# Third attention's scores computed once, masked keys overwritten instead of masked by a matmul, weights in two transfers, and a new order of the stages

## The reference

```python
# layer 0: 16 heads of 16 channels; keys are the 64 context tokens and the 64 latents (x)
h = concat([ctx, x]); q = x @ q_w + q_b; k, v = split(h @ kv_w + kv_b)
attn = where(concat([mask, ones]), q k / 16, -inf)      # masked context keys drop out
x = norm(softmax(attn) v @ out_w + ...) -> gelu MLP -> + x
# layer 1: token-mixing block: layer norm, five mixes, r, k, v, w, g, a scan over the tokens,
#          group norm, output product, a second norm and a gated feed-forward
# layer 2: softmax(q k / 16) over the context, one head, folded weights
# layer 3: 32 query heads of 8 channels, 8 key heads
scores = q k / sqrt(8) + attention_mask; attn = softmax(scores); out = attn v @ Wo + bo
x = layernorm(out + x) * gamma + beta
```

## Time and profile before

| | |
|---|---|
| runs | 1628.13, 1628.97, 1629.14 us, median 1628.97 |
| the profiled execution | 1628.69 us, of which 1626.5 us from the first to the last instruction |
| busy in the span | PE 1459.5 us (90%), DVE 958.1 (59%), ACT 626.7 (39%), POOL 649.4 (40%) |
| granted TensorE clock, mean | 0.964 |
| chain that ended last | PE 71%, DVE 10%, ACT 7%, POOL 7% |

### The profile page before, as it was taken

One profiled execution on the slowest core, in us unless ns is written; L12 is line 12 of the kernel. 1 busy time (PEld: TensorE's weight loads), 2 busy tenths in 40 slices (PEclk: granted clock), 3 DMA queues, 4 the chain that ended last, 5 costly groups with the idle time before them and its releaser, 6 DMA issues.

```text
span 1626.5 us, 45176 instructions
## 1 busy us (share of the span) xinstructions
PE 1459.5 (90%) x19704; PEld 1119.1 (69%) x19704; DVE 958.1 (59%) x1913; ACT 626.7 (39%) x1367; POOL 649.4 (40%) x604
## 2 busy tenths in 40 slices
PE   6777999999999999999999999999899999997664
PEld 4665767777777767777776777777676777775443
DVE  1244576665657576674757666575756656573733
ACT  2332444434343443534344343434344343433221
POOL 1043344525344453525335452533445253443410
PEclk9898999999999999999999999999999999997877
DMA  8021130404022040403113040311304040221300
GB/s 293 11 41 29 22 67 15 77 25 77 25 31 58 16 76 24 77 25 54 34 24 74 18 77 25 70 28 28 65 14 77 25 77 24 34 31 22 49 7 8
DMA packets 83093, 75.27 MB, mean 46 GB/s; under 512 B 37201, under 2 KB 72145, under 8 KB 82513
## 3 DMA queue, kind: packets, MB, share of 16 engines
q1 hardware_dynamic: 82896, 72.39, 22.2%
HBM read 34.61 MB, written 4.19 MB: 24 GB/s over the span
## 4 chain that ended last, share of the span: by engine, by line
PE 71%; DVE 10%; ACT 7%; POOL 7%; issue 3%; DMA 2%; SPq 0%; DVEq 0%; POOLq 0%; ACTq 0%
PE pw L410 21%; PE pw L388 14%; PE pw L394 7%; PE pw L610 6%; PE pw L616 6%; PE pw L559 3%; DVE c L1117 3%; POOL ab L1065 3%; PE pw L513 3%; POOL ab L1029 2%; PE pw L399 2%; PE pw L552 2%; ACT qz L861 2%; PE pw L729 2%; ACT ptC L839 1%
## 5 line engine op out<-in xcount | busy, mean ns | idle before, releaser
L1029 POOL TENSOR_TENSOR ab<-big,kvrg 128x504 f32<-128x504 f32 x128 | 161.2, 1259 | 115.9 <-DMA big<-kvrg 86.3
L1065 POOL TENSOR_TENSOR ab<-ab,kvrg 128x512 f32<-128x512 f32 x128 | 162.7, 1271 | 67.9 <-DVE ab L1262 67.6
L1262 DVE TENSOR_TENSOR_SCAN ab<-pw,ab 128x256 f32<-128x256 f32 x256 | 158.6, 671 | 48.4 <-ACT ab L947 45.9
L1052 POOL TENSOR_TENSOR big<-big,xaB 128x512 f32<-128x512 f32 x80 | 101.4, 1269 | 166.4 <-DVE big L1241 165.2
L610 PE MATMUL pw<-tA,wb 128*128 128x256 f32 x512 | 123.6, 397 | 3.7 <-DVE tA L1206 3.1
L388 PE MATMUL pw<-big,wb 128*128 128x256 f32 x512 | 125.8, 389 | 0.0
L616 PE MATMUL pw<-wb,ptA 128*128 128x256 f32 x512 | 118.1, 384 | 0.0
L1112 DVE TENSOR_REDUCE mx<-pw 128x8 f32<-128x1024 f32 x64 | 75.2, 1216 | 72.3 <-PE pw L410 72.3
L610 PEld LDWEIGHTS pw<-tA,wb 128*128 128x128 f32 x512 | 98.4, 197 | 27.8 <-issue 12.4
L1117 DVE RECIPROCAL a<-pw 128x256 f32<-128x256 f32 x32 | 56.1, 1752 | 103.0 <-PE pw L410 103.0
L616 PEld LDWEIGHTS pw<-wb,ptA 128*128 128x128 f32 x512 | 96.9, 192 | 15.2 <-issue 2.4
(11 more groups left out here) (216 smaller groups left out, 3082.6 us busy)
## 6 DMA issues: line engine op xcount, KB each, us to landing
big<-kvrg SPq DMA_DIRECT2D x256, 128.0 KB, 4.1
hT<-in_h SPq DMA_DIRECT2D x16, 512.0 KB, 4.4
m<-in_amask SPq DMA_DIRECT2D x96, 64.0 KB, 2.3
wb<-in_wb SPq DMA_DIRECT2D x1, 5120.0 KB, 22.6
a<-in_x SPq DMA_DIRECT2D x16, 256.0 KB, 4.2
xB<-in_x SPq DMA_DIRECT2D x16, 256.0 KB, 2.8
result<-c SPq DMA_DIRECT2D x16, 256.0 KB, 2.1
m<-in_mask SPq DMA_DIRECT2D x16, 128.0 KB, 2.5
```

Of the source, the lines that this page charges most:

```text
L1029: G.tensor_tensor(ab[i % 4][:, :, :, 1:S], vx[i % 3].rearrange("p j (b s) -> p j b s", b=NB)[:, :, :, 0:S - 1], k, ALU.mult).then_inc(kv_p ...
L1052: G.tensor_tensor(v, v, xaB[:, :, :, 1:S + 1].rearrange("p k b s -> p (k b) s"), ALU.add).then_inc(xm_ok, 1)
L1065: G.tensor_tensor(ab[i % 4][:, :, :, :], st[i % 2][:, :, :, :], r, ALU.mult).then_inc(pd_ok, 1)
L1262: last = V.tensor_tensor_scan(st[i % 2][:, j, :, :].rearrange("p b s -> p (b s)"), kn(b5)[:, i // 4, :], ab[i % 4][:, j, :, :].rearrange(" ...
```

## The change

1. Third attention: `max1` is as before up to the maxima. Then DVE subtracts the maxima from the scores that lie in SBUF (two instructions of 128x1024 for each pair of sequences). `exp1` no longer computes anything: PE turns the 16 blocks of 128x128 into the four banks (`turn_scores`) and ACT exponentiates as before. The stage `turn1` is gone on PE and ACT. The mask is loaded in one layout (two transfers a tile instead of six), and POOL's maximum over it is a third as large.
2. First attention: the mask matmuls of `max0` are gone. Instead DVE overwrites the masked context keys in `kT` by a latent's key (`copy_predicated`, two a tile) before the scores; `exp0` still removes masked keys by its bias, so only the maximum sees the copies.
3. `v3` is computed once for each sequence instead of twice (8 products instead of 16), and DVE spreads it in 8 copies instead of 4.
4. `mix2`: the two products of a pair are issued one after the other instead of alternating.
5. Weights `wa` in two transfers: the first holds `vec`, `q0`, `k0`, `ident` and small tables, the second (from `v0` on) is issued behind the first context. PE no longer waits for DVE's constants, and `fv` is scaled later.
6. `ORDER` is another string.

```diff
-WEIGHTS_A = [("ident", P), ("q0", 2 * C), ("k0", 2 * C), ("v0", 2 * C), ("o0", 2 * C), ("vec", 64), ("fv", 2 * C), ("ones0", 48), ("ones3", 64), ("pick", 32),
-             ("top", P), ("eye", 32), ("o3", 2 * C)]
+WEIGHTS_A = [("vec", 64), ("q0", 2 * C), ("k0", 2 * C), ("ident", P), ("ones0", 48), ("ones3", 64), ("pick", 32), ("top", P), ("eye", 32),
+             ("v0", 2 * C), ("o0", 2 * C), ("fv", 2 * C), ("o3", 2 * C)]
...
-ORDER = "AABACBABCCBCABCABCABBCBBCABBAABABACBACBCBCBBCCBBACBAABBCABABACBBCBBBCBBBACCBACCBCB"
+ORDER = "ABABBABBBABBABBCBABBABBBBBCACBCBBBCCABBCCACBCBBBCAAACBBBBCABCBACAABCAABBCACCCACCC"
...
-            sp.dma_start(wa[:, :], wa_d).then_inc(ld_w, 16)
+            sp.dma_start(wa[:, 0:ca["v0"][0]], wa_d[:, 0:ca["v0"][0]]).then_inc(ld_w, 16)
             load_context(0)
+            sp.dma_start(wa[:, ca["v0"][0]:na], wa_d[:, ca["v0"][0]:na]).then_inc(ld_v, 16)
...
+            def turn_scores(p):
+
+                for r in range(4):
+                    for k in range(4):
+                        last = nc.tensor.transpose(ps[r][:, k * P:(k + 1) * P], pt[1][p][:, r, k * P:(k + 1) * P], ident)
                 last.then_inc(e_ps, 1)
...
-            def mixes(*js):
-
+            def mix(j):
+
+                f = MIX[j]
+                g = group(f % 4)
                 for m in range(2):
-                    for j in js:
...
+                    last = mm(kn((b4, b5)[j % 2])[:, m, :], w("m2", f // 4)[g, m * P:(m + 1) * P], thB[g, f // 4, :], start=True, stop=True)
+                last.then_inc(m2_ps, 1)
...
                 elif name == "exp1":
+                    pe.wait_ge(s_ok, t * 4 + 2 * i + 2)
                     if i == 0:
-                        pe.wait_ge(m3_ok, t + 1)
-                        pe.wait_ge(mt_sb, TURN[1, t] + 1)
+                        pe.wait_ge(a_rd, t * 4 + 4)
                     else:
                         pe.wait_ge(e_sb, 4 * TURN[1, t] + 2)
-                    exp_scores(1, i)
+                    turn_scores(i)
...
             pe.wait_ge(ld_w, 16)
-            pe.wait_ge(set_pool, 2)
-            pe.wait_ge(set_dve, 7)
...
+                if layer == 1:
+                    for j in range(2):
+                        dve.wait_ge(a_mx, 4 * a + 2 * p + j + 1)
+                        v = src[:, 2 * j:2 * j + 2, :].rearrange("p r (g s) -> p r g s", g=g)
+                        V.tensor_tensor(v, v, mx[:, 2 * j:2 * j + 2, g * p:g * p + g].unsqueeze(3).broadcast_to([P, 2, g, S]), ALU.subtract).then_inc(s_ok, 1)
...
+                    for m in range(2):
+                        last = V.copy_predicated(kT[:, m, :, 0:S], gone[:, :, :], kT[:, m, :, S:S + 1].broadcast_to([P, NB, S]))
+                    last.then_inc(k0_ok, 1)
```

More of the change, by code:

```diff
@@ L52, in attention @@
 def attention(layer):
-    return [(f"{name}{layer}", p) for name, ps in (("max", 2), ("turn", 1), ("exp", 2), ("value", 2), ("out", 2)) for p in range(ps)]
+    return [(f"{name}{layer}", p) for name, ps in (("max", 2), ("turn", 1 - layer), ("exp", 2), ("value", 2), ("out", 2)) for p in range(ps)]
 def scans():
@@ L317, in load_mask @@
             def load_mask(t):
-                for g in range(4):
-                    sp.dma_start(m3[32 * g:32 * g + 32, :, :, :], amask_d[bass.ds(t * NB, NB), :, :].rearrange("b (h x) k -> x b h k", h=2)).then_inc(ld_3, 16)
                 for e in range(2):
-                    sp.dma_start(m3q[S * e:S * e + S, :, :], amask_d[bass.ds(t * NB, NB), :, :].rearrange("b q k -> q b k")).then_inc(ld_3, 16)
+                    sp.dma_start(m3[S * e:S * e + S, :, :], amask_d[bass.ds(t * NB, NB), :, :].rearrange("b q k -> q b k")).then_inc(ld_3, 16)
             def load_x(t, to, which):
@@ L424, in max_scores, with exp_scores @@
                                  kz3[group(r), b, :, :], i == 0, i == 1)
[L425 to L430, removed]
                 last.then_inc(a_ps, 1)
-            def exp_scores(layer, p):
+            def exp_scores(p):
                 for i in range(2):
@@ L438, in exp_scores @@
                         for r in range(4):
[L439 to L451, removed]
+                            into(ps[r][:, (2 * i + j) * P:(2 * i + j + 1) * P], kT[group(r), j, b, :], qz[group(r), j, b, :, :], i + j == 0, False)
@@ L452, in exp_scores @@
                 for i in range(2):
-                    b = 2 * p + i
                     for j in range(2):
                         for r in range(4):
[L456 to L464, removed]
+                            at = 4 * p + 2 * i + j
@@ L567, in part_a @@
                         pe.wait_ge(*read(SLOT["q0", 0, t]))
-                        pe.wait_ge(*read(SLOT["k0", 0, t]))
-                        pe.wait_ge(*read(SLOT["k0", 0, t] + 1))
-                        pe.wait_ge(m0_ok, t * 2 + 1)
+                        pe.wait_ge(k0_ok, t + 1)
                         if a:
@@ L771, in part_c @@
                     for b in range(NB):
-                        for e in range(2):
-                            for c in range(2):
-                                last = mm(bank(k)[64 * e:64 * e + 64, b * 64:(b + 1) * 64], hT[t % 3][:, c, b, 0:S], w("v3", c),
-                                          start=(c == 0), stop=(c == 1))
+                        for c in range(2):
+                            last = mm(bank(k)[64 * (b % 2):64 * (b % 2) + 64, b // 2 * 64:b // 2 * 64 + 64], hT[t % 3][:, c, b, 0:S], w("v3", c),
+                                      start=(c == 0), stop=(c == 1))
                     last.then_inc(full(k)[0], 1)
@@ L992, in part_c @@
                     last.then_inc(read(k)[0], 2)
-                elif name == "turn1":
-                    act.wait_ge(mt_ps, TURN[1, t] + 1)
-                    A(mT[:, :], ps[0][:, 0:P], ACT.Copy).then_inc(mt_sb, 1)
                 elif name == "exp1":
@@ L1335, in part_c @@
                     for e in range(2):
-                        g = slice(64 * e, 64 * e + 64)
-                        for v in range(2):
-                            o = (2 * v + e) * W3
-                            last = V.tensor_copy(v3[g, :, :, v, o:o + W3],
-                                                 bank(k)[g, 0:NT].rearrange("p (b r x) -> p b r x", b=NB, r=2)[:, :, :, o:o + W3])
+                        for h in range(2):
+                            for v in range(2):
+                                o = (2 * v + e) * W3
+                                last = V.tensor_copy(v3[64 * e:64 * e + 64, h:NB:2, :, v, o:o + W3],
+                                                     bank(k)[64 * h:64 * h + 64, 0:P].rearrange("p (b r x) -> p b r x", b=2, r=2)[:, :, :, o:o + W3])
                     last.then_inc(read(k)[0], 2)
@@ L1375, in _ @@
                 c = vec0 + VEC[name][0]
-                V.tensor_scalar(wa[:, c:c + 2], wa[:, c:c + 2], 0.5, None, ALU.mult)
-            V.tensor_scalar(w("fv"), w("fv"), 0.5, None, ALU.mult).then_inc(set_dve, 1)
+                last = V.tensor_scalar(wa[:, c:c + 2], wa[:, c:c + 2], 0.5, None, ALU.mult)
+            last.then_inc(set_dve, 1)
             run(dve, stage)
```

52 lines of the change are left out of this document (29 added, 23 removed).

## The result

The changed kernel takes 1620.64 us (median of 5 runs, 1619.29 to 1623.95), the kernel before took 1629.14 beside it (1628.13 to 1632.06): ratio 0.9941, 95% interval 0.992 to 0.9962. It is faster, by 8.5 us or 0.6%; 1617 had been predicted. The profiled execution took 1620.37 us with a span of 1618.4.

The account below looks back on a forecast made before the run. PE, busy 88.78 of 93.43 us a full round, was taken as the bound. 1628.7 + 3.5 (14 rounds) - 15.6 (start and end) = 1616.6, the median 0.3 above: 1617 us, range 1603 to 1631.

Parts of the forecast that it names:

- the three parts: Full rounds +3.5 us over 14; start and first two rounds -3.6, -1 and -4; last two rounds -4 and -3.
- The round: One full round: PE work 83.9 plus waits 9.5 plus 0.3 is 93.7 us, +0.25; under 92, the waits' list is wrong.
- Third attention: PE's two `exp1` a round, 6.34 us, become 32 turns at 0.11, 3.5 us; with `turn1` gone, -3.0 a round.
- Masks: PE's two mask matmuls of `max0` go: -0.9 us a round.
- v3: PE's `v3`, 1.20 us, becomes half: -0.6 us a round.
- mix2: Products issued one after the other overlap only at the seam: a pair about 1.7 us, +1.5 a round (0 to +1.9).
- Start and end: Program's start and last tiles: earlier PE start -3.6, masks -1, first sum -4, `fk` -4, C alone -3; together -15.6 us.
- The first: The waits don't come in the full rounds: PE idles 7 us a round, round 90.9, time 1578 us; chance 0.2.
- The second: DVE's queue at the round's seam runs 1.9 us later, PE waits 2.75 at `mix1`: +27, 1643 us; chance 0.22.
- The third, the clock: The clock halves behind the turns of `exp1` in each round: +24, 1640 us; chance 0.08.
- The fourth: Turns in long runs take load plus stream, 0.25 us each: +72, 1689 us; chance 0.02.
- The fifth: The program's start and end give nothing: 1632 us; chance 0.03.

Follow-up runs that it names:

- e2: The kernel before with only the new stage order (`turn1` put behind the second `max1`): 1694.39 us, ratio 1.0402 to the kernel before.
- e4: The changed kernel with `wa` in one transfer and PE waiting for the constants, as before: 1621.43 us, ratio 0.9947 to the kernel before the change.

## Why the prediction was right, and where not

**The sum.** 1617 against 1620.6, with the three parts +3.5, -8.6 (start and first two rounds) and -7 (last two) against -6.2, -5.8 and +3.9. The total is right because two errors of some 10 us cancel, and that was luck: the forecast had the whole gain in the start and the end and a small loss in the rounds, while the runs show 6.2 us from the rounds and 1.9 from start and end together.

**The round.** Forecast 93.7 with PE busy near 86 and 8 idle; measured 92.96, 85.64 and 7.32. The round came out 0.47 shorter than before where 0.25 longer was forecast. The forecast named the places of the waits rightly, and most of their sizes. Mean over 13 rounds, forecast in brackets: `value1` 1.11 (1.35), `out1` 0.96 (1.2), `mix1` 0.49 (0.85), `mix2` 1.02 (1.15), `l2s` 0.79 (1.0), `l2p` to `l2o` 0.48 (0.5), `v3` 0.30 (0.4), `zturn` 0.47 (0.85), the sums 1.39 (1.5), `oturn` and `q3` 0.1 (0.7). They come to 7.1. The forecast counted each from the start that PE could have had, which is some 0.16 more than the profile's idle time (at `value1` the 16 turns begin at 699.49 and take 1.74, to 701.23, and the wait ends at 702.51: 1.28 and not 1.11); in that count they are 7.1 + 11 x 0.16 = 8.9 against 9.5, and `zturn`, `oturn` and `q3` are the difference. (For `mix1` the prediction's own times, 13.3 and 12.6, give 0.7 and not 0.85.) PE's work is then 92.96 - 8.9 - 0.3 = 83.8, as forecast (83.9), but not by its parts: `mix2` gave nothing of its +1.5, so the savings beside it were about 3.1 and not 4.5. Taken back one by one they are 3.4, 0.6 and 0.3 of PE's busy time; that is 4.3. The 1.2 between 4.3 and 3.1 is about what the new order costs PE by itself: the old work in it (e2) has 90.17 of busy time against 88.81 in the old one, 1.4 more. The prediction took PE's work to be the same in either order. Which stages the 1.4 lies in isn't shown.

**Third attention.** -3.0 forecast; 3.9 a round when it is taken back, of which 3.4 is PE's busy time. The turns went as said: 1.74 us for 16. DVE went to 67.0 us a round and not 65.5; two small operations that stretch beside POOL are 1.3 of that (last section).

**Masks.** -0.9 forecast; 0.4 to 0.5 in rounds at full clock, below what the medians can tell. I counted both masks as work of their own; in the new order the first adds nothing beside `mix2`, and the second 0.44 us. **v3.** -0.6 forecast, nothing measured: the work came out from in front of a wait. I took PE's work and PE's waits as two sums, but an edit just ahead of a wait on POOL's products takes from the work and gives to the wait: with v3 as before PE idles 6.58 us a round, in the changed kernel 7.02.

**mix2.** This is the term that failed: +1.5 forecast (0 to +1.9), 0 measured, 1.06 us for a pair in either form. I took it that products issued one after the other can only overlap at the seam.

**Start and end.** PE began at 7.08, forecast 6.4, and the first sum of the round of A with B waited 3.76 instead of 8.27, as said, but two later ones waited 2.87 and 1.87. The sums of that round waited 8.5 us in all instead of 11.3. With the one transfer back, the first `k0` stands at 14.2 instead of 10.5 and the third tile's at 159.7 instead of 153.7, but the medians are only 0.8 us apart, and the interval of e4 is 3.3 us to either side: that the 3.7 us arrive at the end is neither shown nor excluded. At the end the forecast was wrong in sign, -7 against +3.9. There A has nothing left to cover with; PE's largest waits in the last two rounds:

```profile
1458.17 2.07 PE L613 MATMUL pw<-tB,wb 128*128 128x256 f32 x4 [4.71 <-DVE tB L1129]
...
1524.57 3.78 PE L395 MATMUL pw<-wb,tB 128*128 128x256 f32 x8 [4.17 <-DVE tB L1267]
...
1550.92 3.78 PE L389 MATMUL pw<-tC,wb 128*128 128x256 f32 x8 [5.36 <-DVE ptC L1129]
...
1592.36 3.65 PE L447 MATMUL pw<-wa,ptC 128*128 128x128 f32 x16 [4.92 <-DVE ptC L1082]
1598.13 3.34 PE L447 MATMUL pw<-wa,ptC 128*128 128x128 f32 x16 [2.12 <-ACT ptC L816]
```

All over 4 us are for DVE: with the subtractions DVE has 8.5 us more there (83.08 against 74.61 in the trace of before). PE's idle gaps in the stretch add up to 54.4 us, 52.3 before. The other half of the 3.9 is PE's busy time, 103.32 against 101.41, although its work is less: the mean granted clock is 0.77 against 0.79. Three of the four runs of 16 turns there fall on a granted clock of 0.50 to 0.57 and take 3.3 to 3.7 us. The four take 13.1 us where the four `exp1` of before took 15.3, so 2.2 is saved where 5.7 would be at full clock. I had `fk` 4 us earlier because norm2 was; its wait is 5.36 instead of 3.16.

**The rivals.** The first (waits don't come, 1578) is out: a round takes 92.96 and not 90.9, and stays above the 92 that the prediction gave as the sign. The second (DVE's queue at the seam, 1643) is out: 0.49 at `mix1` in place of 2.75. The third, the clock, is out: three rounds of 14 show a granted clock under 1.00 (0.96, 0.98, 0.98), and a run of 32 turns keeps 1.00. The Trainium skill's sentence, "TensorE: Matmul & The Clock Gate", Part 4: PE-mode transpose, that such a turn "doesn't count as PE-busy the same way", did not show in these 32-bit turns. The fourth, turns at 0.25 us, is out at 0.107 to 0.110. The Trainium skill, "TensorE: Matmul & The Clock Gate", Part 3: Packing small matmuls — row/col tiling, says that a load overlaps a running matmul only in other rows of the array. The trace does not agree: each turn's load used all 128 rows (128*128 in the row of L447), 31 loads were 3.41 of 3.50 us busy, and the turns still began every 0.11 us. The fifth (start and end give nothing, 1632), which had the least chance but one, is the one whose part came nearest: -1.9 in place of -15.6. The time isn't 1632 only because the rounds gave 6.2 us.

## What to carry to other kernels

Price an edit on the engine that bounds by where it stands: work ahead of a wait on another engine (v3 and the fourth sum) is cover, and taking it out gives nothing. A stage that is moved into a wait must be no longer than the wait, or it delays the part that waits (`l2k`, 1.92 us into 1.02). Moving work from the busiest engine to one in the same strict order needs the order rebuilt around it: the same new work was 1674 us in the old order and 1621 in the new. Where a gain is of the size of what the clock does at the end of the program, read single rounds at a granted clock of 1.00 and not the medians, and take the same kernel's trace twice before a difference at the start or the end is put down to an edit.

## What the runs showed of the hardware

**DVE waits for POOL.** The comparison of the masks took 286 ns before and 875 now, the small one beside it 156 and 838. Timelines of DVE and of POOL at that place:

```profile
715.80 0.99 DVE L1171 TENSOR_SCALAR gone<-m 128x256 int32<-128x256 int32 x1
716.71 1.00 DVE L1172 TENSOR_SCALAR mk<-mkint 64x4 f32<-64x4 int32 x1
```

```profile
715.37 1.27 POOL L1055 TENSOR_TENSOR c<-c,rows 128x512 f32<-128x512 f32 x1
716.60 1.09 POOL L993 TENSOR_TENSOR sxB<-xaB 128x512 f32<-128x512 f32 x1
```

Each of DVE's two ends where a POOL instruction ends or shortly behind (716.79 against 716.64, 717.71 against 717.69), whatever its own size: 64x4 elements take 1.00 us. At the start of the same trace, with nothing on POOL, the same two take 0.29 and 0.15:

```profile
10.76 0.29 DVE L1171 TENSOR_SCALAR gone<-m 128x256 int32<-128x256 int32 x1 [3.33 <-DMA mkint<-in_maskt]
10.96 0.15 DVE L1172 TENSOR_SCALAR mk<-mkint 64x4 f32<-64x4 int32 x1
```

The Trainium skill, "SBUF — State Buffer", SBUF: two separate sides, says that DVE, when it works in a mode with two ports or reads two SBUF inputs, and GpSimd share a pair of ports as an exclusive lock, held for a whole instruction. The rows agree with such a lock; in which mode the two operations ran, no run here shows. In the round shown it costs nothing, as DVE waits 1.23 us for PE behind it.

**Products on different rows of the array** run together however they are issued: eight matmuls of 32 rows, of two products, take 1.06 us from start to start both in alternation and product by product, and the four of a single product take 1.06 as well:

```profile
725.27 1.13 PE L495 MATMUL pw<-thB,wb 32*128 32x256 f32 x4
726.33 1.99 PE L389 MATMUL pw<-big,wb 128*128 128x256 f32 x8
```
